# Splitting the experts' down weights into float16 halves beside the graph layer of a four-block kernel

## The reference, cut to what matters

```python
def _L1_gnn_ref(x, edge_index, W, b):          # the graph layer
    h = jnp.einsum('nd,od->no', x, W) + b
    norm = deg_inv_sqrt[row] * deg_inv_sqrt[col]
    return jax.ops.segment_sum(norm[:, None] * h[col], row, num_segments=num_nodes)

def _L1_ffn_ref(x, w1s, w2s, w3s, W1, W2, W3, Wg):   # the experts
    def geglu(x, w1, w2, w3):
        return jax.nn.gelu(x @ w1, approximate=False) * (x @ w2) @ w3
    shared = geglu(xf, w1s, w2s, w3s)
    idx = jnp.argmax(xf @ Wg, axis=-1)
    for e in range(8):
        y = geglu(xf, W1[e], W2[e], W3[e])
        final = final + jnp.where((idx == e)[:, None], y, 0.0)
    return shared + final
x = x + _L1_gnn_ref(_layernorm(x, axis=-1), edge_index, L1_gnn_W, L1_gnn_b)
x = x + _L1_ffn_ref(_layernorm(x, axis=-1)[None], ...)[0]
```

## Time and profile before

| what | us |
|---|---|
| three timed runs, median (lowest to highest) | 2593.78 (2592.81 to 2595.72) |
| span of the profiled execution, first to last instruction | 2589.7 |
| graph layer, first phase, about | 2083 to 2206.6 |
| graph layer, second phase | 2206.6 to 2310 |
| shared expert, about | 2310 to 2415 |
| 17 slots | 2415 to 2589.7 |

### The profile page before, as it was taken

How to read it: one execution, slowest core, us unless ns; L and a number is a source line. 1 busy time by engine, 2 the same in 40 slices (tenths; PEclk the granted TensorE clock), 3 DMA queues, 4 the chain that set the end, 5 groups by cost and what they waited for, 6 DMA issues and landing times. The chain is left out here.

```text
span 2589.7 us, 34729 instructions
## 1 busy us (share of the span) xinstructions
PE 2465.5 (95%) x12652; PEld 1666.1 (64%) x12652; DVE 1968.1 (76%) x2504; ACT 1230.4 (48%) x1413; POOL 143.8 (6%) x173
## 2 busy tenths in 40 slices
PE   6999299889999999999999999999999989999998
PEld 4666287756666666666666666666666556568776
DVE  7876799798888897797797788788788756665422
ACT  6322676565555455445545545545544235522111
POOL 1000000010000000000000000000000011000222
PEclk9999699989999999999999999999999999999999
DMA  5211311143232232322421422422331045836993
GB/s 164 63 39 39 67 40 40 67 141 62 73 63 57 75 61 57 88 49 55 95 57 41 96 56 41 96 56 47 88 105 49 1 136 178 264 135 211 353 379 109
DMA packets 145389, 252.12 MB, mean 97 GB/s; under 512 B 67128, under 2 KB 82106, under 8 KB 138838
## 3 DMA queue, kind: packets, MB, share of 16 engines
q1 hardware_dynamic: 135378, 231.40, 31.3%
q0 software_dynamic: 4928, 10.25, 1.6%
q10 hardware_dynamic: 4932, 8.30, 0.9%
HBM read 204.01 MB, written 49.33 MB: 98 GB/s over the span
## 5 line engine op out<-in xcount | busy, mean ns | idle before, releaser
L1761 PE MATMUL wide_ps<-keep_own_room,rails_hid_hi 128*125 128x512 f16 x4200 | 1250.7, 379 | 5.2 <-DVE rails_hid_lo L1478 3.2
L1761 PE MATMUL wide_ps<-keep_own_room,rails_hid_lo 128*125 128x512 f16 x2100 | 796.4, 379 | 0.0
L1761 PEld LDWEIGHTS wide_ps<-keep_own_room,rails_hid_hi 128*125 128x125 f16 x4200 | 564.7, 137 | 312.5 <-issue 6.4
L1761 PEld LDWEIGHTS wide_ps<-keep_own_room,rails_hid_lo 128*125 128x125 f16 x2100 | 286.9, 137 | 167.0 <-issue 0.6
L1253 ACT ACTIVATE rails_hid_hi<-rails_raw_a,keep_scale_hidden 128x1000 f16<-128x1000 f32 x210 | 274.5, 1334 | 209.5 <-DVE rails_raw_a L1497 90.8
L1478 DVE SCALAR_TENSOR_TENSOR rails_hid_lo<-rails_raw_a,keep_scale_hidden,rails_hid_hi 128x1000 f16<-128x1000 f32 x210 | 312.1, 1516 | 41.7 <-ACT rails_hid_hi L1253 41.6
L1243 ACT ACTIVATE rails_raw_a<-wide_ps,keep_scale_gelu 128x1000 f32<-128x1000 f32 (+1 forms) x192 | 181.6, 951 | 323.6 <-PE wide_ps L1746 320.2
L1532 DVE SCALAR_TENSOR_TENSOR keep_X<-wide_ps,rails_out_scale,keep_X 125x1024 f32<-125x1024 f32 x180 | 198.6, 1103 | 132.3 <-PE wide_ps L1761 132.3
L1486 DVE SCALAR_TENSOR_TENSOR keep_own_room<-carried_w_land,rails_w_scale,keep_own_room 128x2048 f16<-128x2048 f32 x105 | 246.0, 2343 | 0.7 <-ACT keep_own_room L1268 0.7
L1268 ACT ACTIVATE keep_own_room<-carried_w_land,rails_w_scale 128x2048 f16<-128x2048 f32 x105 | 208.9, 1990 | 9.8 <-DVE carried_w_land L1516 5.7
L1228 ACT ACTIVATE rails_raw_a<-carried_w_land 128x2048 f32<-128x2048 f32 x64 | 121.7, 1902 | 141.9 <-DMA carried_w_land<-cproj 141.7
(11 more groups left out here) (476 smaller groups left out, 3359.3 us busy)
## 6 DMA issues: line engine op xcount, KB each, us to landing
carried_w_land<-cproj SPq DMA_DIRECT2D x79, 1024.0 KB
ffn_w_up<-split_d SPq DMA_DIRECT2D x9, 2048.0 KB
keep_own_room<-W SPq DMA_DIRECT2D x11, 1024.0 KB, 5.8
ffn_w<-W SPq DMA_DIRECT2D x11, 1024.0 KB
rails_xs<-xt_d SPq DMA_DIRECT2D x124, 78.1 KB
keep_comb_hi<-W SPq DMA_DIRECT2D x8, 1024.0 KB, 7.2
split_d<-graph_high SPq DMA_DIRECT2D x16, 512.0 KB, 6.6
keep_X<-split_d SPq DMA_DIRECT2D x4, 2048.0 KB
```

The source lines that it names most:

```text
L1761: mm = nc.tensor.matmul(ps[0:P, t, :], hid[(q + b) % 2][l][:, k, t * P:(t + 1) * P], w[(q + b) % 2][r][:, k, :], start=(k == 0 and i == 0) ...
```

## The change

W3 of each of the eight routed experts becomes a part like W1 and W2, so there are 24 parts and not 16. Parts 0 to 15 are W1 and W2 as before; 16 to 23 are W3, stored in a second scratch array `split3_d`. `sum_at(i)` becomes `4 * i // 3`: three parts in four steps, with sums in steps 0, 1, 2, 4, 5, 6, 8 and so on, so that the last sum stays in step 30. The loads of the counts are queued at other places. In the slots the gate is now scaled by a power of two for each token (its largest absolute value is found, from which two factors are made), is turned, and is split in a high and a low half; the down product is 12 float16 matmuls in place of 4 float32 ones; and the copy of the result multiplies it by a scale for each token.

```diff
     RING = 3
     LANDS, HIGHS = 3, 3
-    PARTS = 2 * EXPERTS
-    OWN_AT = 15
+    PARTS = 3 * EXPERTS
+    UPPERS = 2 * EXPERTS
+    OWN_AT = PARTS - 1
...
         def sum_at(i):
 
-            return 2 * i
+            return 4 * i // 3
...
-                    sp.dma_start(land[b], routed[i % 2][i // 2].rearrange("(p a) f -> p (a f)", p=128)).then_inc(part_in[b], 16)
+                    sp.dma_start(land[b], part_of(i).rearrange("(p a) f -> p (a f)", p=128)).then_inc(part_in[b], 16)
...
-                later = {6: 3, 7: 4, 8: 5, 12: 6, 13: 7, 14: 8, 15: 9}
+                later = {8: 3, 10: 4, 11: 5, 17: 6, 19: 7, 20: 8, 22: 9}
...
-                    sp.dma_start(w3[s % DOWNS], downs[expert_of(s)]).then_inc(down_in[s % DOWNS], 16)
+                    sp.dma_start(w3[s % DOWNS].rearrange("p n k d -> p (n k d)"), split3_d[expert_of(s)]).then_inc(down_in[s % DOWNS], 16)
...
-                        nc.scalar.copy(gt[u % 2][:], ps_g[u % 2]).then_inc(gt_set, 1)
+                        nc.scalar.copy(gt[u % 2]["hi"][:], ps_g[u % 2]).then_inc(gt_set, 1)
...
-                        nc.vector.scalar_tensor_tensor(gate_f[u % 2][:], gelu_f[u % 2][:], slot_scale["gate"][:, s:s + 1],
-                                                       ps_b[u % 2][:, 0:INTER], ALU.mult, ALU.mult).then_inc(gate_set, 1)
+                        nc.vector.scalar_tensor_tensor(gelu_f[u % 2][:], gelu_f[u % 2][:], slot_scale["gate"][:, s:s + 1],
+                                                       ps_b[u % 2][:, 0:INTER], ALU.mult, ALU.mult).then_inc(g_step, 1)
+                        dve.wait_ge(g_step, 5 * s + 1)
+                        nc.vector.tensor_reduce(g_peak[:], gelu_f[u % 2][:], AX.X, ALU.max, apply_absolute_value=True).then_inc(g_step, 1)
...
+                        nc.vector.tensor_scalar(gate_f[u % 2][:], gelu_f[u % 2][:], g_up[:, 0:1].bitcast(F32), None, ALU.mult).then_inc(gate_set, 1)
...
-                        nc.vector.tensor_copy(res[s % 2][:, cols], ps_y[:, h, :]).then_inc(y_taken, 1)
+                        nc.vector.tensor_scalar(res[s % 2][:, cols], ps_y[:, h, :], g_down[:, s:s + 1], None, ALU.mult).then_inc(y_taken, 1)
...
                 for s in range(SLOTS):
+                    g_lo(TILES + s)
                     if s + 2 < SLOTS:
                         x_lo(TILES + s + 2)
...
-                    pe.wait_ge(gt_set, u + 1)
+                    pe.wait_ge(gt_lo_set, u + 1)
                     pe.wait_ge(down_in[s % DOWNS], 16 * (s // DOWNS + 1))
...
-                            mm = nc.tensor.matmul(ps_y[:, h, :], gt[u % 2][:, k, :], w3[s % DOWNS][:, k, h * BANK:(h + 1) * BANK],
-                                                  start=(k == 0), stop=(k == 1))
+                            for n, (l, r) in enumerate(SPLIT):
+                                part = 0 if r == "hi" else 1
+                                mm = nc.tensor.matmul(ps_y[:, h, :], gt[u % 2][l][:, k, :], w3[s % DOWNS][:, part, k, h * BANK:(h + 1) * BANK],
+                                                      start=(k == 0 and n == 0), stop=(k == 1 and n == 2))
```

More of the change, by code:

```diff
@@ L1834, in graph_layer @@
 def graph_layer(nc, X, mean_var, rstd, ident, w_land, w_part, row, scales, counts, dis, indeg, combs, stat_parts, std, eps,
-                own, own_scales, Wg, w1s, w2s, w3s, routed, split_two, split_d, spare):
+                own, own_scales, Wg, w1s, w2s, w3s, routed, split_two, split_d, split3_d, spare):
     RING = 3
     LANDS, HIGHS = 3, 3
-    PARTS = 2 * EXPERTS
-    OWN_AT = 15
+    PARTS = 3 * EXPERTS
+    UPPERS = 2 * EXPERTS
+    OWN_AT = PARTS - 1
     HALF_T = TILES // 2
@@ L2352, in _, with experts @@
                     add_low(j, 1)
-def experts(nc, X_all, mean_var, rstd, std, eps, stat_parts, ident, own_w1g, own_w2, own_w3, up_room, w3_room, own_scales, split_two, split_d, W3, xn_d, out):
+def experts(nc, X_all, mean_var, rstd, std, eps, stat_parts, ident, own_w1g, own_w2, own_w3, up_room, w3_room, own_scales, split_two, split_d, split3_d, xn_d, out):
     TE = [P, TILES, EXPERTS]
@@ L2388, in experts @@
         own_gt = {n: c.sb(f"own_gt_{n}", [128, TILES, 2, P], F16) for n in ("hi", "lo")}
-        gt = [c.sb(f"gt{k}", [128, 2, SLOT], F32) for k in range(2)]
+        gt = [{n: c.sb(f"gt_{n}{k}", [128, 2, SLOT], F16) for n in ("hi", "lo")} for k in range(2)]
         xg = [c.sb(f"xg{k}", [SLOT, DIM], F32) for k in range(XG)]
@@ L2411, in experts @@
         counted = c.sb("counted", [128, EXPERTS, EXPERTS], F32)
-        place1, place2, place3, place4 = [c.sb(f"place{k}", TE, F32) for k in range(1, 5)]
+        place2, place3, place4 = [c.sb(f"place{k}", TE, F32) for k in range(2, 5)]
+        place1 = is_best
         pos, pos_i = c.sb("pos", [P, TILES], F32), c.sb("pos_i", [P, TILES], I32)
@@ L2754, in _ @@
                                               ALU.is_equal))
-                for kind in ("gelu", "gate"):
+                for kind in KINDS:
                     last = nc.vector.tensor_tensor(scale_of[kind][:], is_chosen[:], bc(slot_scale[kind][:, 0:EXPERTS], [128, EXTRAS, EXPERTS], 1),
@@ L2951, in program @@
         own_scales = {n: keep.sb(f"own_{n}", [128, 1], F32) for n in ("gelu", "gate", "out")}
-        split_two = keep.sb("split_two", [128, 2 * EXPERTS], I32)
+        split_two = keep.sb("split_two", [128, 3 * EXPERTS], I32)
         early = ctx.enter_context(ExitStack())
@@ L2973, in program @@
         graph_layer(nc, X, mean_var, rstd, ident, w_land, w_part, row, next_scales, counts, dis, indeg, combs, stat_parts, std, eps,
-                    own, own_scales, Wg, w1s, w2s, w3s, (W1, W2), split_two, split_d, spare)
+                    own, own_scales, Wg, w1s, w2s, w3s, (W1, W2, W3), split_two, split_d, split3_d, spare)
         early.close()
         recycle(nc)
-        experts(nc, X_all, mean_var, rstd, std, eps, stat_parts, ident, shared_w1, shared_w2, shared_w3, own_room, comb_hi, own_scales, split_two, split_d, W3, xn_d, out)
+        experts(nc, X_all, mean_var, rstd, std, eps, stat_parts, ident, shared_w1, shared_w2, shared_w3, own_room, comb_hi, own_scales, split_two, split_d, split3_d, xn_d, out)
 def kernel(x, src, dst, L0_gnn_W, L0_gnn_a_l, L0_gnn_a_r, L0_ffn_rail_maker, L0_ffn_rail_up_proj, L0_ffn_w_cproj,
```

47 lines of the change are left out of this document (31 added, 16 removed).

## The result

The changed kernel takes 2643.09 us (median of four runs, 2640.28 to 2646.21), the kernel before 2593.44 in the same comparison: 1.0188 times as long, interval 1.0175 to 1.0202, or +49.7 us. The forecast was 2604, +10. The profiled execution of the kernel after spans 2643.7 us, 54.0 more than that of before. First the three rows of the kernel before that the front part doesn't have: the last closing product of the graph layer, the shared expert's first turn, and the matmuls that place the tokens in slots, near the end of the shared expert.

The account below looks back on a forecast made before the run. It took PE to bound the slots and a loop through ACT and DVE the graph layer's first phase. -14.4 (down products) + 20.3 (layer) + 0.3 + 0.3 + 4 (scatters) = +10.5 on 2593.8: 2604 us, range 2588 to 2617.

Parts of the forecast that it names:

- Do the loads keep up?: Graph layer, first phase: a landing buffer's store and load take 9.1 us, within the loop's shortest gap of 10.5.
- rival 2: Loads bind the graph layer, each step waiting for a landing: layer +28, in all 2612 us; chance 0.13.
- Second phase ... I count 0.5: Graph layer, second phase: PE's pace stays and the end has room, so it costs only 0.5 us.
- the cover that I had named: Graph layer's end: the shared weights waited for the last store until 2283.34, while the phase ends at about 2310.
- The loop: Graph layer, first phase: ACT and DVE wait for each other; +3.6 us a pair of tiles, closing product +19.8.
- The 7.7 for the start: Graph layer's start: new sum, scale and the wait behind POOL's fetch delay `xt_lo` of tile 3 by 7.7 us.
- the maximum on POOL: Graph layer, first phase: the later sum's maximum finds DVE's low half done and takes 0.35 us, not 1.19: -0.9.
- the rival length of 1.19: Graph layer: if 1.19 us were the maximum's own length, a pair costs 4.5 and the sum 2.8 us more.
- the give-back: Slots: down products save 14.4 us on PE, less 0.3, 0.3 and 4 us; bounds of the slots -14 to -8.
- 4 us on the scatters by way of the copy: Slots 7 to 12: DVE's result copies wait for scatters, so PE waits some 4 us; bounds 0 and 8.
- rival 3: Scatters bind the slots from slot 5 on: 7.3 us lost and not 4, so 2607 us; chance 0.15.

Follow-up runs that it names:

- four landing buffers: Changed kernel with four landing buffers for the parts in place of three: 2630.78 us, 1.0143 against the kernel before.
- short loads: Changed kernel, but from part 3 on a load brings 128 of the 2048 columns of a part: 2611.84 us, 1.0073 against the kernel before.
- the slots alone: Graph layer of the kernel before with the slots of the changed kernel, reading W2's halves in place of W3's: 2590.29 us, 0.9986 against the kernel before.
- the gathers first: Layer of before, changed slots reading W2's halves; POOL issues the gather of slot s + 5 ahead of the scatter of slot s: 2588.51 us, 0.9978.
- the run with few bytes: Layer of before, changed slots reading W2's halves; up loads from slot 7 and down loads from slot 5 bring a quarter of their bytes: 2581.14 us, 0.9947.
- four buffers and the scale moved: Changed kernel with four landing buffers, and DVE makes a part's scale behind `mixed` in the layer's first phase: 2618.25 us, 1.0091 against the kernel before.

## Why the prediction was wrong

**The step that failed** is "Do the loads keep up? ... That holds, by 1.4 us". I had added a low store's 3.3 us and a load's 5.8, medians of the kernel before, and set the 9.1 against a gap of 10.5. In the tiles of that kernel SP issues a low store some 7 us behind the high one, so mostly alone. Its high stores, issued some 1.5 us behind a load, showed already what a store takes there, twice as long, and my sum left that out:

```profile
split_d<-graph_high SPq DMA_DIRECT2D x16, 512.0 KB, 6.6
```

With three parts in four steps the low store comes close behind a load and a high store too, and takes 8.6 in the turn shown above. The sum should have been made for the queue in its new state: load, high store and low store one after another, some 9.5 us from load to load, each load then waiting for the low store just ahead of it. I had the mechanism as rival 2, with a chance of 0.13, and priced it at 28 us for the layer; it is 56. The price was short because I saw one place in which late loads cost time, ACT's sums in the tiles. The runs show two more in this kernel, the issue of the shared weights and the last store at the layer's end; with four landing buffers the fetch becomes another.

**"Second phase ... I count 0.5"** failed for the same reason. From the first closing product to the shared expert's first turn 20 us more were lost. 12.5 of them lie ahead of the last closing product, in a stretch in which ACT's sums wait 24.2 of the 40.2 us for loads, and 7.4 behind it: the cover that I had named, the shared weights waiting until 2283.34 with the phase's end at 2310, was used up, and what it costs then I had not priced.

**The loop was right**, and only the runs with short loads show it: 19.1 us at the closing product against 19.8, 10.4 over three pairs of tiles against 11.1, DVE's wait for POOL before the scale of part 2 4.62 us against 4.1 (4.43 in the kernel after). The 7.7 for the start holds 1 us that none of its terms gives: 2.0, 0.45, 4.1 and 0.2 make 6.75, and 6.7 is what the run has. Of the maximum on POOL the forecast held too: 0.35 us in most steps of the kernel after, 1.28 at 2132.74, beside DVE's low half of 2131.45 to 2133.80. The rule of the Trainium skill ("SBUF — State Buffer", Who interferes with whom) fits both. By the rival length of 1.19 the closing product would have been 22.6 us late, and the short loads have 19.1.

**In the slots** the down product (2.59) and the slot (8.95) were right, the give-back was too small. I had put 4 us on the scatters by way of the copy; lost were 14.4 - 4.1 = 10.3 in the slots of the whole change, 9.8 in the slots alone. Of the 10.3, 9.0 lie between the products of slots 4 and 10 (62.7 against six times 8.95). I had left out the gathers: PE's wait for them is no row of the trace of before, and I did not bound it. They are not the whole of it, since with the gathers first PE waits for none of them and no clear gain came of it. The mechanism was rival 3's, full DMA engines: two slots take 20.6 to 21.1 us, as in the rows 20.57, and the run with few bytes gives nearly all of it back. Before the change the scatter of slot 9 took about as long:

```profile
2523.16 1.59 POOL L2538 DMA_INDIRECT out<-ffn_res,ffn_tokens  x1 [7.61 <-DVE ffn_res L2676]
```

The copy that waited for it began at 2541.62, 18.5 us later; in the kernel after it is 18.4 to 18.8. So a scatter did not grow, as I had worked out from the Trainium skill ("DMA: Bandwidth & Descriptors", Queues, rings and completion order), by which a DMA engine takes turns between the queues that have work. It does not help: a scatter of 18.5 us is longer than two slots of PE, 17.9, and the slots of that stretch run at its pace.

**What stays open.** How the 37.7 us of the layer divide among these places is not settled: with one relieved the others grew, so their shares don't add. From the marks of the kernel after against those of the short loads the sum builds up as 17.8 by the first closing product, 12.5 more to the last, 7.4 to the shared expert. Of the 17.8, none lies ahead of tile 3, 7.1 in the six tiles (91.2 against 84.0), and 11 behind them. A version with all places relieved at once was not tried. Nor was a third result buffer in the slots.

## What to carry to other kernels

Work that is "hidden beside" a stage has three covers to be reckoned with: the engines' idle time, the links by which two engines wait for each other, and the queue of transfers. For the queue, don't add the times of single transfers from a trace in which they run apart; line up what one turn of the loop issues, and ask which wait in the program's order comes right behind the transfer that it waits for. And where a stretch shows the DMA engines at 1.0, a faster PE need gain nothing: here the six slots in the middle became 3.9 us slower, and what was gained came ahead of them and behind them. The same splitting, done where it moves no bytes, came out some 53 us better.

## What the runs showed of the hardware

**Issuing a load can hold up ACT for as long as 8.7 us.** The two 1 MB loads of the shared expert's weights took 2.02 and 2.44 us to issue before the change, 5.42 and 3.04 after. Before, and then with four buffers and the scale moved:

```profile
2211.04 2.02 ACTq L2013 DMA_DIRECT2D carried_w_land<-w2s  x1
2213.09 2.44 ACTq L2013 DMA_DIRECT2D carried_w_land<-w3s  x1
```

```profile
2229.93 8.73 ACTq L2025 DMA_DIRECT2D carried_w_land<-w2s  x1
2238.68 2.94 ACTq L2025 DMA_DIRECT2D carried_w_land<-w3s  x1
```

Nothing in the program makes ACT wait there. In all, the two take 4.5 us before the change, 5.5 with short loads, 8.5 in the kernel after and 11.7 with four buffers; what holds the issue up, no run shows.

**PE can pay twice for a wait.** After 7.65 and 5.71 us of idleness the turns at 2174.94 and 2206.52 took 1.90 us, where one that follows on work takes 1.02 and one after 1.64 us of idleness 1.04. The window of 2160 to 2180 has a mean granted clock of 0.83, a part of it at the lower of the two levels:

```profile
2174.94 1.90 PE L2291 MATMUL graph_ps_x<-keep_ident,graph_xn 125*128 125x125 f32 x8 [7.65 <-DVE graph_xn L2089]
...
2206.52 1.90 PE L2291 MATMUL graph_ps_x<-keep_ident,graph_xn 125*128 125x125 f32 x8 [5.71 <-DVE graph_xn L2089]
```

```profile
2160.00:2180.00 20.00, 12.35 (x52) 8.01 (x51) 8.19 (x15) 11.94 (x12) 0.70 (x2) 0.83 0.65 197
```

The first turn of the shared expert is no clear case: it took 1.93 us after 10.81 us of idleness, but 1.93 as well after 3.47 in the slots alone, and 1.27 after 3.47 before the change. My sums had PE at its full pace behind every wait.
